# Normalisation, modulation and the splitting of maxima moved between the engines of a four-layer transformer kernel, with a new order of its steps

## The reference, cut to what matters

```
def _ln(x):
    mu = jnp.mean(x, axis=-1, keepdims=True)
    var = jnp.var(x, axis=-1, keepdims=True)
    return (x - mu) * jax.lax.rsqrt(var + EPS)      # normalise
...
xm = _ln(x) * (1.0 + sc_sa) + sh_sa                 # modulate, one scale and shift per sequence and channel
qkv = (xm @ qkv_w + qkv_b).reshape(B, N, 3, H, HD)
...
attn = jnp.einsum('bhnd,bhsd->bhns', q, k) * SCALE
attn = jax.nn.softmax(attn, axis=-1)                # subtracts each row's maximum
```

## Time and profile before

| | |
|---|---|
| median of 3 runs | 1740.38 us |
| the profiled execution | 1737.27 us, of which its span 1735.5 us |
| granted clock of TensorE, mean | 0.997 of full speed |
| PE busy | 1629.4 us, 94% |
| PEld busy | 1392.2 us, 80% |
| ACT busy | 1500.9 us, 86% |
| DVE busy | 1477.8 us, 85% |
| POOL busy | 834.0 us, 48% |
| DMA | mean 24 GB/s |

### The profile page before, as it was taken

One profiled execution on the slowest core, in us unless ns is written; L12 is line 12 of the kernel. 1 busy time (PEld: TensorE's weight loads), 2 busy tenths in 40 slices (PEclk: granted clock), 3 DMA queues, 4 the chain that ended last, 5 costly groups with the idle time before them and its releaser, 6 DMA issues. The chain is left out here.

```text
span 1735.5 us, 75191 instructions
## 1 busy us (share of the span) xinstructions
PE 1629.4 (94%) x31141; PEld 1392.2 (80%) x31141; DVE 1477.8 (85%) x4368; ACT 1500.9 (86%) x3896; POOL 834.0 (48%) x1591
## 2 busy tenths in 40 slices
PE   5988999999999999999999999999999999999998
PEld 4767788878888888878888888888888877877887
DVE  6888888988988888888888889888899898899865
ACT  3777898989998999999898988899898988888996
POOL 4434444544545454554454545444555454545441
PEclk9999999999999999999999999999999999999999
DMA  7000000000000000000000000000000000000000
GB/s 235 3 21 3 18 24 24 18 21 12 24 24 24 24 9 18 24 24 24 19 9 24 24 24 24 24 3 24 24 24 24 24 15 18 18 15 15 3 6 16
DMA packets 57792, 41.27 MB, mean 24 GB/s; under 512 B 13552, under 2 KB 56176, under 8 KB 57328
## 3 DMA queue, kind: packets, MB, share of 16 engines
q1 hardware_dynamic: 57456, 36.46, 7.4%
HBM read 31.99 MB, written 4.46 MB: 21 GB/s over the span
## 5 line engine op out<-in xcount | busy, mean ns | idle before, releaser
L1263 DVE TENSOR_REDUCE top<-half 128x32 f32<-128x2048 f32 x160 | 364.9, 2281 | 33.6 <-PE half L969 31.9
L1457 ACT ACTIVATE pT<-half 128x512 f32<-128x512 f32 x640 | 329.4, 605 | 40.6 <-PE half L997 38.7
L786 POOL TENSOR_TENSOR rstd<-shifted,minus_halves 128x2 f32<-128x2 f32 x256 | 183.1, 715 | 291.6 <-DVE shifted L1235 288.9
L1492 ACT ACTIVATE pT<-half,mod 128x64 f32<-128x64 f32 x896 | 195.2, 350 | 11.3 <-PE half L1093 9.8
L969 PE MATMUL half<-k_heads,q_heads 32*128 32x128 f32 x5120 | 186.9, 282 | 8.8 <-DVE kvT L1133 3.4
L814 POOL TENSOR_TENSOR top<-top 128x32 f32<-128x32 f32 x160 | 39.2, 245 | 311.9 <-DVE top L1263 311.5
L1441 ACT ACTIVATE v_cols<-half 64x128 f32<-64x128 f32 x640 | 175.2, 274 | 14.7 <-PE half L956 8.1
L1133 DVE TENSOR_SCALAR nT<-half,mod 128x64 f32<-128x64 f32 x640 | 172.2, 332 | 18.1 <-PE half L846 17.5
L1430 ACT ACTIVATE k_heads<-half,key_bias,own_head_sb 128x256 f32<-128x256 f32 x320 | 163.7, 572 | 25.4 <-PE half L949 23.9
L969 PEld LDWEIGHTS half<-k_heads,q_heads 32*128 32x128 f32 x5120 | 159.8, 188 | 32.3 <-issue 21.8
L1012 PE MATMUL half<-pT,v_cols 128*32 128x64 f32 x10240 | 176.0, 220 | 7.8 <-ACT pT L1457 3.6
(11 more groups left out here) (150 smaller groups left out, 3850.4 us busy)
## 6 DMA issues: line engine op xcount, KB each, us to landing
gates<-gate_store SPq DMA_DIRECT2D x128, 128.0 KB, 3.1
x_rows<-x SPq DMA_DIRECT2D x32, 128.0 KB, 2.8
c_rows<-context SPq DMA_DIRECT2D x32, 128.0 KB, 2.1
out<-n_rows SPq DMA_DIRECT2D x32, 128.0 KB, 1.9
w_sb<-weights SPq DMA_DIRECT2D x1, 1856.0 KB, 7.8
w_sb<-weights SPq DMA_DIRECT2D x2, 512.0 KB, 6.4
logit_bias<-logit_store SPq DMA_DIRECT2D x64, 1.5 KB, 3.5
row_sb<-rows SPq DMA_DIRECT2D x1, 769.5 KB, 8.2
```

The lines of the kernel that those rows point to most:

```text
L786: nc.gpsimd.tensor_tensor(rstd[s][:, :], shifted[s][:, :], minus_halves[:, 0, :], ALU.pow).then_inc(rstd_in[s], 1)
L1263: nc.vector.tensor_reduce(term[s][0], halves[HALF_OF[n]][:, :, :].rearrange("p g (c k) -> p g c k", k=SEQ), AX.X, ALU.max).then_inc(tops_r ...
L1457: nc.scalar.activation(turn_cols[s][:, g, :], halves[HALF_OF[n]][:, g, :], ACT.Exp, scale=ATT_SCALE).then_inc(scores_read, 1)
L1492: m = nc.scalar.activation(dst, src[:, at], ACT.Silu, bias=mod[s][:, k, tb:tb + 1])
```

## The change

Three edits, and new strings for the order.

1. **Normalising.** VectorE normalises both rows tiles, by two scalar-tensor-tensor instructions, (x - mean) x rstd, in which rstd is a tensor operand spread over 128 columns (L1224 of the kernel after). ScalarE's activation and GpSimd's `minus` are gone; TensorE waits for one event instead of two.
2. **Modulating.** Two tensor-tensor instructions over all 256 columns: a multiplication that writes back into the same PSUM bank (step `cols` or `kvnorm`, L1234 for the first), and an addition into `nT` or `kvT` (new steps `shift` and `kvshift`, L1238). The bank comes free with the addition. The two steps have places of their own in the order, and the second waits for the first.
3. **Splitting.** The two subtractions run on VectorE (new steps `split` L1266 and `split_low` L1270), each with its own place in the order; `lows` on TensorE waits for a semaphore of the stream (`tops_split[s]`).
4. **Order.** `SEQUENCE` has 4946 characters in place of 4434, all of them new; in `HALVES` the first ten change.

```diff
@@ -137,7 +137,7 @@
-    return [("q", a), ("k", a), ("v", a), ("tops", None), ("lows", None), ("scores", None),
+    return [("q", a), ("k", a), ("v", a), ("tops", None), ("split", None), ("split_low", None), ("lows", None), ("scores", None),
@@ -151,7 +151,7 @@
-    before = [("kvnorm", kv)] if kv else []
+    before = [("kvnorm", kv)] + ([("kvshift", kv)] if isinstance(kv[1], tuple) else []) if kv else []
@@ -160,7 +160,7 @@
-    return [("normal", None), ("cols", how)]
+    return [("normal", None), ("cols", how)] + ([("shift", how)] if isinstance(how, tuple) else [])
@@ -209,54 +209,59 @@
 SEQUENCE = (
-    "f21022200011122220000f0f20023f0101112210f2333014f23114443330000f421002222f0001031f02202222f111102f02"
...
+    "2f01f222000210020200101222f0402010012012f1210f212f013121002033031f1f1f02132301322303f0302420004120f1"
...
@@ -335,12 +340,12 @@
-                if side == FOR_VECTOR and kind == "l3_scores":
+                if side == FOR_VECTOR and kind in ("cols", "kvnorm", "l3_scores"):
                     pending[s] = fills[side]
...
-        if kind == "l3_below":
+        if kind in ("shift", "kvshift", "l3_below"):
@@ -784,8 +787,6 @@
                         nc.gpsimd.tensor_tensor(rstd[s][:, :], shifted[s][:, :], minus_halves[:, 0, :], ALU.pow).then_inc(rstd_in[s], 1)
-                        count.next(rstd_in[s])
-                        nc.gpsimd.tensor_scalar(minus[s][:, :], moments[s][:, 1, 0:1], -1.0, rstd[s][:, 1:2], ALU.mult, ALU.mult).then_inc(minus_in[s], 1)
@@ -807,14 +808,6 @@
-                    if kind == "tops":
-
-                        maxima += 1
-                        pool.wait_ge(tops_read, maxima)
-                        nc.gpsimd.tensor_tensor(term[s][1], term[s][0], upper[s][0], ALU.subtract).then_inc(pool_own, 1)
-                        count.next(pool_own)
-                        nc.gpsimd.tensor_tensor(term[s][2], term[s][1], upper[s][1], ALU.subtract).then_inc(tops_split, 1)
@@ -1133,13 +1118,6 @@
-                def modulate(dst, src, s, how):
-
-                    for tb in range(GROUP):
-                        m = nc.vector.tensor_scalar(dst[:, tb, :], src[:, tb * SEQ:(tb + 1) * SEQ], mod[s][:, how[0], tb:tb + 1],
-                                                    mod[s][:, how[1], tb:tb + 1], ALU.mult, ALU.add)
-                    return m
@@ -1236,17 +1220,30 @@
                     if kind == "normal":
                         count.next(rstd_in[s])
-                        nc.vector.tensor_scalar(n_rows[s][:, 0, :], x_rows[s][:, 0, :], moments[s][:, 0, 0:1], rstd[s][:, 0:1],
-                                                ALU.subtract, ALU.mult).then_inc(rows_normed[s], 1)
+                        for t in range(2):
+                            m = nc.vector.scalar_tensor_tensor(out=n_rows[s][:, t, :], in0=x_rows[s][:, t, :], scalar=moments[s][:, t, 0:1],
+                                                               in1=rstd[s][:, t:t + 1].broadcast_to([D, D]),
+                                                               op0=ALU.subtract, op1=ALU.mult)
+                        m.then_inc(rows_normed[s], 1)
...
-                        modulate(nT[s], banks.take(), s, arg).then_inc(v_emptied, 1)
+                        held[s] = banks.take()
+                        makes("scaled", s, nc.vector.tensor_tensor(bank4(held[s]), bank4(held[s]), over_tokens(mod[s][:, arg[0], :]), ALU.mult))
+
+                    if kind == "shift":
+                        after("scaled", s)
+                        nc.vector.tensor_tensor(nT[s][:, :, :], bank4(held[s]), over_tokens(mod[s][:, arg[1], :]), ALU.add).then_inc(v_emptied, 1)
...
+                        made["maxima", s] = tops_read, attended
+
+                    if kind == "split":
+                        after("maxima", s)
+                        makes("middle", s, nc.vector.tensor_tensor(term[s][1], term[s][0], upper[s][0], ALU.subtract))
+
+                    if kind == "split_low":
+                        after("middle", s)
+                        nc.vector.tensor_tensor(term[s][2], term[s][1], upper[s][1], ALU.subtract).then_inc(tops_split[s], 1)
@@ -1409,11 +1415,6 @@
-                    if kind == "normal":
-                        count.next(minus_in[s])
-                        nc.scalar.activation(n_rows[s][:, 1, :], x_rows[s][:, 1, :], ACT.Identity, scale=rstd[s][:, 1:2],
-                                             bias=minus[s][:, :]).then_inc(rows_normed[s], 1)
```

More of the change, by code:

```diff
@@ new lines @@
+    "1223021322402f0321031304340123f14111001322040ff001f0440232041f330023100512443301223033014010f0044021"
+    "4011001230212141130310121301001531201210151131210300341301100013010122004114010022120001332032113411"
+    "0232131001420103102000010003120010422101200010134140252442130305421002400001301130302220102111212212"
+    "0100002154101133021230100200320102113034103010203230250301144112004113421310154553212152225313312542"
+    "3242242355421252133542343514142341330415432104542325150233525113050113531052431052530431523204010511"
@@ new lines @@
+    "4141302421541423555042443013521342530240031403030234533452540433300230254220225535254415454533254434"
+    "5504002324532505244120405400415250542044022350432155110143215023521221150100121215022353311350445341"
+    "4245334441054550441513354550154041533105035130302535041315100150350541531312513031341030241314025455"
+    "2001055430331252352300351512502233321223414504104045444251214251045041305204214320111541250402410041"
+    "3453041030300153425321020321024102120421425421124214052340143012543033543042244544245144245551301003"
@@ L499, in build @@
         shifted, rstd = each("shifted", [D, 2]), each("rstd", [D, 2])
-        minus = each("minus", [D, 1])
         c_shifted, c_rstd, c_minus = each("c_shifted", [D, 2, 2]), each("c_rstd", [D, 2, 2]), each("c_minus", [D, 2, 2])
@@ L574, in build @@
         a_filled, a_emptied = sem("a_filled"), sem("a_emptied")
-        tops_filled, tops_read, tops_split = sem("tops_filled"), sem("tops_read"), sem("tops_split")
+        tops_filled, tops_read, tops_split = sem("tops_filled"), sem("tops_read"), [sem(f"tops_split{s}") for s in range(STREAMS)]
         scores_filled, scores_read = sem("scores_filled"), sem("scores_read")
@@ L586, in build @@
         sums_inverted, o_weighed = [sem(f"sums_inverted{s}") for s in range(STREAMS)], [sem(f"o_weighed{s}") for s in range(STREAMS)]
-        minus_in = [sem(f"minus_in{s}") for s in range(STREAMS)]
         p3_done, p3_normed = [sem(f"p3_done{s}") for s in range(STREAMS)], [sem(f"p3_normed{s}") for s in range(STREAMS)]
@@ L753, in _ @@
             def _(pool):
-                count, rows_made, maxima = Counted(pool), 0, 0
+                count, rows_made = Counted(pool), 0
                 nc.gpsimd.memset(minus_halves[:, :, :], -0.5).then_inc(consts_made, 1)
@@ L921, in _ @@
                     if kind == "cols":
-                        count.next(rows_normed[s], 2)
+                        count.next(rows_normed[s])
                         if isinstance(arg, tuple):
@@ L978, in _ @@
                             pe.wait_ge(of_keys_in, 4 + STREAMS)
-                        after("tops", s)
+                        count.next(tops_split[s])
                         nc.tensor.transpose(to_a.slot()[:, 0:D // 2].bitcast(BF16), uppers[s], ident_half[:, :]).then_inc(a_filled, 1)
@@ L1245, in _ @@
                             copy_mods(n, 0, M_L1Q)
-                        modulate(nT[s], banks.take(), s, arg).then_inc(v_emptied, 1)
-                    if kind == "kvnorm" and isinstance(arg[1], tuple):
-                        modulate(kvT[s], banks.take(), s, arg[1]).then_inc(v_emptied, 1)
+                        held[s] = banks.take()
[3 more added lines that the diff above has]
+                        nc.vector.tensor_tensor(nT[s][:, :, :], bank4(held[s]), over_tokens(mod[s][:, arg[1], :]), ALU.add).then_inc(v_emptied, 1)
+                    if kind == "kvnorm" and isinstance(arg[1], tuple):
+                        held[s] = banks.take()
+                        makes("scaled", s, nc.vector.tensor_tensor(bank4(held[s]), bank4(held[s]), over_tokens(mod[s][:, arg[1][0], :]), ALU.mult))
+                    if kind == "kvshift":
+                        after("scaled", s)
+                        nc.vector.tensor_tensor(kvT[s][:, :, :], bank4(held[s]), over_tokens(mod[s][:, arg[1][1], :]), ALU.add).then_inc(v_emptied, 1)
                     if kind == "q":
```

89 lines of the change are left out of this document (41 added, 48 removed).

## The result

| | before | after |
|---|---|---|
| median | 1740.05 us (16 runs) | 1736.49 us (16 runs) |
| ratio, 95% interval | | 0.9974 (0.9962 to 0.9986) |
| profiled span | 1735.5 us | 1734.4 us |

The forecast gain (1724 us, -16 us) didn't come: the kernel became 3.6 us faster. Of the prediction's cases it was the second, "it cancels", that happened.

The account below looks back on a forecast made before the run. The prediction took TensorE, 94% busy with 106 us idle in short handovers, as the bound. Path terms -22 + 18 - 13 + 20 - 5 - 3 = -5 us and order -11 made -16: 1740.4 to 1724 us, range 1693 to 1760.

Parts of the forecast that it names:

- it cancels: Rival for the whole kernel: path terms give -5 us, the order nothing, longer-held banks take some back; 1738 us, chance 0.25.
- What bounds the kernel: TensorE, 94% busy, leaves 106 us in many short handovers; VectorE's time priced at 34%, ScalarE's at 11%.
- Modulation: VectorE's two 256-column instructions at 414 ns replace four of 64 columns: -48 us of VectorE, -22 us on the path.
- Normalising: VectorE's pair at 600 ns: +54 us of VectorE, +18 us on the path.
- The port: Rival: VectorE's two-input normalising instructions stall on GpSimd, 788 ns a pair, 1740 us; chance counted within the cancelling case's 0.25.
- Overlap: VectorE gets 192 more instructions whose ends overlap: -8 us of its busy time, -3 us on the path.
- ScalarE: ScalarE, freed of normalising, gets 114 us back; at 11% that is -13 us on the path.
- Splitting: 320 subtractions move to VectorE at 189 ns: +60 us, +20 us on the path, less 5 us of TensorE's waits.
- The order: New queue order takes 10% of TensorE's 106 us idle time, a chosen figure: -11 us, bounds 0 and -27.
- The rival that VectorE becomes the bound: VectorE's queue, at 89% of the old span, delays what TensorE needs: +20 us, 1760 us, chance 0.22.

Follow-up runs that it names:

- the first experiment: Instructions of before in the order of after: 1880.0 us against before's 1740.4; instructions of after in the order of before: 1819.3 us.
- the added wait: After, with GpSimd's wide `lifted` operations waiting for the last normalisation ahead of them in the order: 1715.4 us against 1736.5 without it.

## Why the prediction was wrong, step by step

- **What bounds the kernel.** Right that TensorE's 106 us of idle time are all there is, made of many short handovers. Wrong in the price derived from it: VectorE's time was valued at its 34% share of the last quarter's chain. In after the chain can be followed over the whole span, and there VectorE has 38%:

```profile
PE 45%; DVE 38%; ACT 7%; issue 5%; POOL 2%; DMA 2%; SPq 1%; DVEq 0%; POOLq 0%; ACTq 0%
```

  Neither share is the price. Measured with the order of before kept, it was 0.57 to 0.66 us per us. With the order of after kept it was 0.67 for the modulation and near 0.9 for whatever shortened the pair (tensor-scalar form, GpSimd's work left out, GpSimd's wait), and the splits, moved back, even gave the opposite sign. So no single price holds. A share of the chain counts the places where VectorE is last now; a longer instruction also makes it last in places where it wasn't.
- **Modulation.** Right to the microsecond in VectorE's time (-48 us). On the path -22 us forecast; alone in the old order it gave -23, and undoing it in the new order cost 35. The nearest row with a PSUM input was the right one to take for the durations.
- **Normalising.** This is the step that failed. "600 ns a pair, +210 ns, x 256 = +54 us of VectorE" holds for the 146 pairs beside which GpSimd does nothing wide (601 ns). The other 110 took 1217 ns, and all together made +121 us. The rival "The port" described this mechanism and priced the pair at 788 ns and 1740 us; it was counted as a part of the cancelling case, with "GpSimd's work falls by 18%" against it. But none of the change's cuts to GpSimd's work was a wide instruction: what went were `minus` (128 x 1) and the subtractions (128 x 32). The bound of +102 us was also too narrow, since it took the old instruction's mean of 394 ns, and the pair's instructions came to 473. With 121 in place of 54 the prediction's own sum gives -16 + 67 x 0.34 = +7 us: this step alone uses up the forecast gain. The rule of the Trainium skill ("GPSIMD Engine Reference", "1. Specifications": contention of GpSimd with VectorE's two-port and two-input instructions) was the one to weigh more. The traces agree with it in both forms, 473 and 457 ns in the mean, though not for every GpSimd instruction: the power, 706 ns long, holds nothing up. On the other rule that the prediction drew on ("VectorE: DVE Perf Modes", "Mode 2×_2P": two results a cycle for a tensor-scalar between SBUF tiles) the least duration of 243 ns, which the prediction took as agreeing, decides nothing, since scalar-tensor-tensor reaches 248 ns. What does agree is the rest behind a wide GpSimd instruction, 82 ns in the median for tensor-scalar and 149 for the other form. Undisturbed, it is worth 10 ns a pair.
- **Overlap.** Forecast -8 us of VectorE's busy time. The three parts measured -48 + 121 + 64 = +137 us and the whole grew by 83, so the overlap took -54. The short subtractions lie largely within their neighbours' ends: undoing them takes 64 us of their own busy time away and 39 us off VectorE's. At 34% this gives 16 us back, and ScalarE's smaller relief takes 3: the prediction's sum with every busy time put right is -6 us. That this is near the measured -4 says nothing for its prices, as the points on the price and on the order show.
- **ScalarE.** -89 us of busy time where -114 was forecast: what it gave back on the path was not measured by itself. In the new order its half of the rows would come late (85.7 us of waits in the first experiment), and the normalisation on VectorE takes that wait away.
- **Splitting.** +64 us of VectorE (60 forecast). On the path +36 us in the old order, where +15 was forecast; in the new order the same edit is worth -9 us.
- **The order.** "10% of TensorE's 106 us", chosen, -11 us. With the instructions of after it is worth -83 us (1819.3 to 1736.5), and with those of before it costs 140 us. It doesn't add to the edits as a term of its own; it fits one set of durations and producers. The edits were forecast at -5 and cost +79, the wrong sign; the order was forecast at -11 and gave -83. Their sum came out near zero. That the total landed in the range was luck of two errors of opposite sign.
- **The rival that VectorE becomes the bound.** Busy share 90%, as it said, yet 39 us less of its work by the undone splits made nothing faster. So its busy time by itself is not the bound; that the latency of single handovers is, is the likely reading and was not measured by itself.

Left open: how the 21 us of the added wait divide between the pair's own stretch and what stands behind it in VectorE's queue; and what an order searched with the collision in its durations would give. No such search was made.

## What to carry to other kernels

An order that is searched for a set of durations can't be priced apart from them: ask what the edits cost in the old order and what the order gives to the new instructions, and expect large terms of opposite sign. Price an instruction by its median and its tail apart, and look in the timeline at what the tail runs beside; moving a second such instruction to the same engine may more than double the exposure. Before explaining encounters by the order of the queues, count how many would happen by chance. Where two engines collide, a wait that delays the uncritical job can be worth more than the edit itself.

## What the runs showed of the hardware

- VectorE's normalising pair, inputs and output in SBUF, takes 601 ns by itself, 601 beside a GpSimd power of 128 x 2 elements (706 ns long in the median), and 1060 beside one instruction of 128 x 256. Scalar-tensor-tensor and tensor-scalar are both held.
- An instruction of the pair that starts while a wide GpSimd instruction runs ends a fixed time after that one: 149 ns in the median for scalar-tensor-tensor (120 of 122 between 146 and 154), 82 ns for tensor-scalar (112 of 116 between 80 and 88).
- A tensor-tensor instruction that writes in place to its PSUM bank takes 421 ns for 256 columns, one that writes to SBUF 412: no difference that matters.
- Even a small two-input instruction has the tail: L1270, 128 x 32 elements, took 184 ns in the median and 1029 at most; all 9 of its instructions over 300 ns ran beside a wide GpSimd instruction:

```profile
L1270 DVE TENSOR_TENSOR top<-top x160: 126/184/1029, 22.2 to 1667.4; 128x32 f32<-128x32 f32 x160
```
